# Gated attention with its projections and maxima spread over the units, and experts in groups of four

## What is computed

```python
# second layer: 8 heads (H), 5 gates (E) of which the best 3 (K) count, 64 wide
ss, sd = sigmoid(x @ Ws), sigmoid(x @ Wd)            # (b, t, H, E)
ms, md = _topk_mask(ss, K), _topk_mask(sd, K)
q = einsum('bthed,bthe->bhtd', (x @ Wq), sd * md)
k = einsum('bthed,bthe->bhtd', kv[:, :, 0], ss * ms)
v = einsum('bthed,bthe->bhtd', kv[:, :, 1], ss * ms)
attn = softmax(einsum('bhid,bhjd->bhij', q * scale, k))
out = einsum('bhij,bhjd->bihd', attn, v)
o5 = einsum('bthd,dm->bthm', out, Wo).reshape(b, t, H, E, DIM)
y = einsum('bthem,bthe->btm', o5, md)
# fourth layer: 16 experts (E), each takes its 32 best tokens of a batch
vals, idx = top_k(softmax(x @ Wg + bg, over the tokens), 32)
tok = x[bidx, idx]
h = relu(einsum('bekd,edo->beko', tok, w1) + b1)
h = relu(einsum('bekd,edo->beko', h, w2) + b2)
h = einsum('bekd,edo->beko', h, w3) + b3
y = zeros.at[bidx, idx].add(h * vals)
```

## Time and profile before

| what | us |
|---|---|
| median of 3 runs | 4802.87 |
| the 3 runs | 4802.52 to 4806.01 |
| the profiled execution, its own time | 4799.74 |
| its span, first to last instruction | 4798.0 |
| gated stage, first matmul to last vector instruction | 1327.1 to 2804.5 |
| units of the gated stage, from the first exponential | 1420.4 to 2756.1 |
| expert stage | 4615 to 4798 |

### The profile page before, as it was taken

The page is one execution under the profiler, slowest core; times in us unless marked ns, Lnnn a source line. Parts: engine busy times, 40 slices in busy tenths (PEclk is TensorE's granted clock), DMA queues, the critical chain, the costliest instruction groups (busy, mean ns, idle before and its releaser), DMA issues. The chain is left out here.

```text
span 4798.0 us, 63558 instructions
## 1 busy us (share of the span) xinstructions
PE 4155.6 (87%) x22714; PEld 2198.2 (46%) x22714; DVE 3469.9 (72%) x5821; ACT 1959.7 (41%) x3371; POOL 2801.1 (58%) x2036
## 2 busy tenths in 40 slices
PE   5999999999778898888899848999999999999947
PEld 3544454444355554454554424444444444444416
DVE  3777877877577766766776537887888788788735
ACT  2444443434355454454444313443444344444411
POOL 1655555556536775775776815665666566566710
PEclk6999999999979999999999859999999999999976
DMA  2000000000011000010000021211221112111020
GB/s 50 13 13 13 22 13 22 22 1 5 5 65 34 17 31 20 26 34 17 22 33 1 5 57 25 39 27 27 37 39 27 27 38 38 27 32 31 14 62 18
DMA packets 98042, 125.91 MB, mean 26 GB/s; under 512 B 28896, under 2 KB 76448, under 8 KB 97728
## 3 DMA queue, kind: packets, MB, share of 16 engines
q1 hardware_dynamic: 97728, 121.86, 11.7%
HBM read 103.69 MB, written 18.12 MB: 25 GB/s over the span
## 5 line engine op out<-in xcount | busy, mean ns | idle before, releaser
L777 POOL TENSOR_TENSOR s_psum_p<-s_psum_p,s_prob 128x1024 f32<-128x1024 f32 (+3 forms) x640 | 1350.5, 2110 | 415.5 <-ACT s_prob L524 376.7
L524 ACT ACTIVATE s_prob<-s_sT 128x1024 f32<-128x1024 f32 (+2 forms) x896 | 836.7, 934 | 970.5 <-DVE s_sT L658 478.5
L432 PE MATMUL s_pv<-s_prob,s_vp 128*64 128x512 f32 (+3 forms) x3584 | 888.9, 575 | 3.9 <-POOL s_prob L762 3.0
L777 POOL TENSOR_TENSOR s_psum_p<-s_prob 128x1024 f32<-128x1024 f32 (+1 forms) x128 | 286.9, 2241 | 573.7 <-ACT s_prob L524 571.0
L1657 POOL TENSOR_TENSOR s_psum_p<-s_psum_p,s_prob 128x1024 f32<-128x1024 f32 x192 | 464.2, 2417 | 197.1 <-ACT s_prob L1386 195.9
L663 DVE RECIPROCAL s_recip<-s_recip 128x128 f32<-128x128 f32 x512 | 481.1, 942 | 99.1 <-ACT s_recip L474 99.1
L388 PE MATMUL s_mx<-s_bh,s_ah 64*128 64x512 f32 (+3 forms) x1792 | 390.2, 430 | 183.4 <-DVE s_bm L599 84.5
L609 DVE CUSTOM_DVE_ANT_0 s_mx<-s_mx,s_strip 128x512 f32<-128x512 f32 x640 | 429.4, 712 | 111.8 <-PE s_mx L388 110.8
L1386 ACT ACTIVATE s_prob<-s_sT 128x1024 f32<-128x1024 f32 x256 | 262.7, 1026 | 451.9 <-PE s_sT L1243 451.8
L407 PE MATMUL s_sT<-s_ah,s_bh 64*128 64x512 f32 (+3 forms) x1792 | 414.4, 459 | 19.2 <-ACT s_prob L524 18.9
L599 DVE TENSOR_REDUCE s_bm<-s_mx 128x8 f32<-128x1024 f32 (+3 forms) x384 | 362.4, 944 | 48.9 <-PE s_mx L388 40.0
...
## 6 DMA issues: line engine op xcount, KB each, us to landing
...
```

The source lines that it names most:

```text
L432: last = mm(pv[heads(hd), lo:CH], vp[:, g % 2, j, heads(hd)], prob[:, k % PR, hd, lo:CH], start=j == 0, stop=end)
L524: nc.scalar.activation(prob[:, k % PR, :, lo:CH], sT[:, k % 2, :, lo:CH], ACT.Exp, scale=st.scale).then_inc(exp_done, 1)
L777: nc.gpsimd.tensor_tensor(out[:, :, lo:CH], src, p[:, :, lo:CH], ALU.add)\
```

## The change

**Gated stage.** A pair's 16 projection steps now stand in twelve units: two in each of units 0 to 3, one in each of units 4 to 11. The maxima stand beside them: one chunk in units 4 to 9, two in 10 and 11, three in 12 and 13. The first step of a unit always borrows; a chunk beside a step always uses `s_mx`. Every unit now has at most one job of the shared bank: item in 0 to 3, zt in 4 and 11, rs in 5 and 10, the batch's jobs in 6 to 9 and 12 to 15; zp moves from units 4 to 7 to units 7 to 10. The gates of batches 2 and 3 are computed one pair earlier (pairs 3 and 7 in place of 4 and 8). The layer norm's first three steps move to the end of the pair before. ScalarE scales a unit's first step ahead of the copy of `s_pv`.

**Expert stage.** Four experts at a time, with layers one group apart, eight buffers for the hidden values, and the third layer's matmuls in another order (batch outside, expert inside). `m_res`, its high and its low part are made for each group, and all of `m_place` beside the experts. The scatter is turned around: `m_rhi` and `m_rlo` are the weights and 512 columns of `m_place` stream past, 16 matmuls a batch, which gives the result transposed; ScalarE copies it to `m_xT` and 8 transposes turn it back. In the layer norm, ScalarE squares and sums (8 activations a batch), VectorE centres into `m_xout`, and the scaling of a batch stands behind the centring of the next. The copy to `m_xhi` moves behind the exponential.

```diff
-        self.mx_steps = [0] * 8 + [3, 3, 3, 3, 2, 2, 0, 0]
+        self.mx_steps = [0] * 4 + [1] * 6 + [2, 2, 3, 3, 0, 0]
+        self.pj_steps = [2] * 4 + [1] * 8 + [0] * 4
...
-        if g + 2 < self.GP:
-            for n in range(2 * NB):
-                out[n // 2].append(("pj", g + 2, n))
...
-            for k, u in enumerate((0, 1, 3, 4)):
-                out[u].append(("item", g + 1, k))
+            for k in range(4):
+                out[k].append(("item", g + 1, k))
...
-            out[3].append(("zt", g - 1, 1))
-            for i in range(4, NB):
-                out[i].append(("zp", g - 1, i))
+            out[4].append(("zt", g - 1, 1))
+            out[5].append(("rs", 2 * g - 1))
+            for i in range(4, NB):
+                out[3 + i].append(("zp", g - 1, i))
...
+        gated, ranked = {0: 1, 3: 2, 7: 3}.get(g), {1: 1, 4: 2, 8: 3}.get(g)
...
-            for n in range(7):
-                out[1 + n].append(("ln", b - 1, n))
+        for n, (of, u) in enumerate(((1, 13), (1, 14), (1, 15), (2, 2), (2, 3), (2, 6), (2, 7))):
+            if p == of and b > 0:
+                out[u].append(("ln", b - 1, n))
...
+                early = 1 if steps else 2
+                for t in chunks[:early]:
+                    maxima(t[1], t[2], second(todo, t, k))
                 if k >= 2:
                     values(k - 2)
-                for t in steps[1:2]:
-                    if t[0] == "pj":
-                        project(t[1], t[2])
+                for t in steps[1:]:
+                    project(t[1], t[2])
...
+            def third_layer(q):
+                pe.wait_ge(l2d, 4 * q + 4)
+                for b in range(B):
+                    for e4 in range(4):
+                        e, at = 4 * q + e4, q % 2 * CH + b * P
+                        last = mm(big[32 * e4:32 * e4 + 32, q // 2, at:at + P],
+                                  h2[:, e % 8, 32 * b:32 * b + 32], w3[:, e, :], start=True, stop=True)
...
+                        mm(big[:, b % 2, cols], rhi[:, eg, b, :], place[b][:, eg, cols], start=eg == 0, stop=False)
+                        last = mm(big[:, b % 2, cols], rlo[:, eg, b, :], place[b][:, eg, cols], start=False,
+                                  stop=eg == EG - 1)
...
+                for i in range(NB):
+                    last = nc.scalar.activation(h1[:, i, :], xnew[:, b % 2, i, :], ACT.Square,
+                                                bias=sums[:, b % 2, 0, i:i + 1],
+                                                accum_out=sums[:, b % 2, 1, i:i + 1])
```

More of the change, by code:

```diff
@@ L1290, in _ @@
                     misc_job(t)
-                for t in steps[2:]:
+                for t in chunks[early:]:
                     maxima(t[1], t[2])
@@ L2030, in _ @@
-                last.then_inc(y_full, 1)
+                    if i % 4 == 0:
+                        pe.wait_ge(yT_done, 2 * b + i // 4 + 1)
+                    last = nc.tensor.transpose(turned(b)[:, i * P:(i + 1) * P], xT[:, b % 2, i * P:(i + 1) * P],
+                                               cst.ident[:, :])
+                last.then_inc(t_full, 1)
+            first_layer(0)
+            for q in range(EG + 1):
+                if q + 1 < EG:
+                    first_layer(q + 1)
+                if q < EG:
+                    second_layer(q)
+                if q > 0:
+                    third_layer(q - 1)
@@ L2032, in _ @@
+            pe.wait_ge(rlo_done, EG)
+            for b in range(B + 1):
+                if b < B:
+                    scatter(b)
+                if b > 0:
+                    turn_back(b - 1)
         @block.scalar
@@ L2144, in _, with scale @@
+            def scale(b):
+                dve.wait_ge(rstd_done, b + 1)
+                dve.wait_ge(centred, b + 1)
+                v.tensor_tensor(xout[:, b % 2, :, :], xout[:, b % 2, :, :], wide(rstd[:, b % 2, :]), ALU.mult)\
+                    .then_inc(ln_done, 1)
+            for b in range(B):
+                centre(b)
+                if b > 0:
+                    scale(b - 1)
+                variance(b)
+            scale(B - 1)
         @block.gpsimd
```

311 lines of the change are left out of this document (162 added, 149 removed).

## The result

| | before | after |
|---|---|---|
| median | 4804.4 us (4 runs) | 4693.6 us (4 runs, 4691.3 to 4700.0) |
| ratio, 95% interval | | 0.977 [0.975, 0.979] |
| profiled execution, its span | 4798.0 | 4693.4 |
| last exponential to the end of the gated stage | 48.4 | 53.3 |
| last `m_tok` to the end of the span | 107.5 | 60.7 |

The forecast was 4683 us, within 4640 and 4755. The spans differ by 104.6 us: 57.6 in the gated stage, 47 behind the last `m_tok`. Forecast were 78 and 42. So a difference of a few us in one pair between two profiles is not read as an effect here.

What follows compares the result with a forecast made beforehand. Before, TensorE filled a pair's first half, with holes in the second; after, the borrowed-buffer chain and double chunks bound plain pairs. Gated stage 78 plus expert stage 42 gave 120 us: 4802.9 - 120 = 4683, range 4640 to 4755.

Steps and rivals of the forecast that it cites:

- A plain pair, 78.7: Gated stage, pair without a batch's jobs: unit times sum to 78.7 us, against 81.4 before, a gain of 2.7.
- The chain of 4.5 us: Gated stage, one-step units: scores, exponential, ScalarE's and VectorE's parts through the borrowed buffer set 4.5 us, above TensorE's 4.0.
- The waits at the shared bank: Gated stage, pairs 4 to 13: TensorE's waits of 2.92 and 1.94 us at a second shared-bank job in a unit go.
- The last gates' steps 2 or 3: Gated stage, a batch's jobs: the last gates' steps estimated at 2 or 3 us, bounds 0 and twice that.
- Gates' first steps 6, layer norm 3 and 5, y and gt 1: Gated stage, estimates: sigmoid and first gates' steps 6 us (pairs 0, 3, 7); layer norm 3 or 5; y 1; gt 1.
- Pair 14, 58: Gated stage, pair 14: 58 us, before 69.9, a gain of 12; the wait of 12.89 behind GpSimd's power goes.
- Pair 15 and the end, 0: Gated stage, pair 15 and the end: bound by GpSimd before and after, gain 0.
- Expert stage, 42: Expert stage: 44 us gained, 42 taken; scatter starts 22.0 us after the last `m_tok` instead of 39.3, gaining 17.
- I take full clock: Expert stage, scatter: matmuls at full clock, 0.23 us each rather than 0.43, since TensorE rests only 3 us before.
- the chain longer than 4.5: Rival, chance 0.14: one-step units exceed 4.5 us because VectorE comes late; gated stage hardly gains, 4761 us.
- the longest `zp` each time: Rival, chance 0.06: each `zp` of units 7 to 10 takes 3.02 us, costing 7.6 a pair; 4789 us.
- TensorE did not become the bound: Rival, chance 0.10: TensorE becomes the gated stage's bound, readers keep up, pairs take 73 to 74 us; 4613 us.

## Why the prediction held, and where its steps were off

The time was 11 us above the forecast, well within the range. By the profiled executions 104.6 of the 120 us came: 20 less than forecast in the gated stage, 5 more in the expert stage. The two halves miss in opposite directions, so the sum is nearer than the gated stage's own forecast, and that is luck.

- **A plain pair, 78.7.** Right: 79.9 and 78.5. In pair 11 units 0 to 3 gave 5.6 each (5.7), units 4 to 9 28.8 (29.8; 30.2 in pair 2), 10 and 11 12.9 (12.2), 12 and 13 9.9 (9.4). The chain of 4.5 us was read rightly off and the earlier trace rows. `zp` in units 7 to 9 cost nothing (4.5 each, not 5.0).
- **Where that gain comes from.** The prediction laid it to the new spread and to one shared-bank job a unit. The spread turned back costs 0 to 5 us. The rest came with the places of the jobs (118 and 24 us lost when they are turned back, the first in a harder case than before) and with ScalarE's order, by the estimate above up to 12 us, which the prediction had no term for. How it divides between these was not measured.
- **The waits at the shared bank.** Direction right, size low. I took the 1.9 and 2.9 us of the earlier trace rows as what a doubled unit loses. With old places in the changed kernel it is 4.8 on average; in the kernel before, unit 3 took 8.2 to 10.0 us, 2.6 to 4.4 more than its 5.6 after: the scores, ScalarE and GpSimd behind them come late as well.
- **"The last gates' steps 2 or 3".** This term failed. Against the kernel with these steps taken apart they cost 11.4, 9.9 and 11.8 us in pairs 1, 4 and 8, and 4.2, 2.6 and 3.3 in pairs 0, 3 and 7, which the next term covers. The forecast asked how much VectorE work there was and not in which unit it stood; unit 14, ahead of two steps, has no slack. Pairs 0 to 3 took 13 us more than forecast, pairs 4 to 11 7 more, chiefly through it.
- **Gates' first steps 6, layer norm 3 and 5, y and gt 1.** Pairs 3 and 7 came at 86.0 and 85.1 for 85 (83.3 and 81.8 with the top steps out of them), pairs 5 and 9 at 82 for 82; the norm in 6 and 10 cost 1.5 and not 5.
- **Pair 14, 58.** It took 59.7, in part for the reason given: the norm's power no longer stands behind three gathers. But the wait of 12.89 us that was to go is still 5.38, and only 2.6 us of what it lost are shown to hang on the places of a pair's late jobs, `zp` among them.
- **Pair 15 and the end, 0.** Right as a sum only: up to its last exponential pair 15 became 5.3 us shorter, and the tail behind it 4.9 us longer. The prediction saw neither.
- **Expert stage, 42.** It gave 47. Up to the scatter 19.0 us and not 22: the third layer took 1.08 us a group and not 3.06, and VectorE's 18.6 became the bound. The Trainium skill (TensorEngine Tiling (Array Packing), "Key Properties") says that different tiles can run matmuls in parallel, and the trace agrees; but the order of the loops that lets them was worth 0.8 us in the stage, not 3. "I take full clock" was wrong for twelve matmuls, 2.4 us; a batch took 6.0 and not 6.4, a square with its sum 0.39 and not 0.42.
- **The rivals.** Neither the chain longer than 4.5 nor the longest `zp` each time came in general; stretching like the latter's happens, but to the top steps, in a few units. TensorE did not become the bound here (plain pairs of 73 to 74); it did once the chunk borrowed (73.6). The scatter was slow for twelve of its matmuls.
